# Routed expert layer: the first 128 picks of each expert in a tile of fixed weight address, overflow tiles through buffers that GpSimd fills

## What is computed

```python
def _moe(x2d, Wg, Wu, Wd, cw):
    g = jnp.einsum('th,ehi->eti', x2d, Wg)
    u = jnp.einsum('th,ehi->eti', x2d, Wu)
    a = jax.nn.silu(g) * u * cw.T[:, :, None]
    return jnp.einsum('eti,eih->th', a, Wd)
```

## Time and profile before

| | |
|---|---|
| median of 3 runs | 1508.38 us (1502.71 to 1508.43) |
| the profiled execution | 1497.24 us, its span 1495.4 us |
| PE busy over the span | 1141.3 us (76%) |
| DVE busy | 1062.4 us (71%) |
| ACT busy | 761.0 us (51%) |
| POOL busy | 647.7 us (43%) |
| mean granted clock of PE | 0.776 of full speed |

### The profile page before, as it was taken

One profiled execution on the slowest core, in us unless ns is written; L12 is line 12 of the kernel. 1 busy time (PEld: TensorE's weight loads), 2 busy tenths in 40 slices (PEclk: granted clock), 3 DMA queues, 4 the chain that ended last, 5 costly groups with the idle time before them and its releaser, 6 DMA issues.

```text
span 1495.4 us, 31927 instructions
## 1 busy us (share of the span) xinstructions
PE 1141.3 (76%) x11430; PEld 730.5 (49%) x11430; DVE 1062.4 (71%) x2436; ACT 761.0 (51%) x1506; POOL 647.7 (43%) x707
## 2 busy tenths in 40 slices
PE   5820677777763899996599982888888989996998
PEld 3510455555542322324478761555555665653565
DVE  7886122222257999996788859888888857658785
ACT  4446111111131889884245433989899943334432
POOL 5877000000053110400233335889988856774262
PEclk9955999999996555556699995555555579998999
DMA  9922222222231689894287723898998921111010
GB/s 360 410 122 96 70 65 64 62 65 64 57 124 43 127 176 183 171 182 108 64 211 198 200 54 80 129 149 151 153 152 152 143 61 59 53 44 43 11 33 29
DMA packets 401927, 176.41 MB, mean 118 GB/s; under 512 B 364912, under 2 KB 383600, under 8 KB 399344
## 3 DMA queue, kind: packets, MB, share of 16 engines
q1 hardware_dynamic: 395680, 158.79, 46.4%
q0 software_dynamic: 4800, 13.11, 2.9%
q10 hardware_dynamic: 1296, 2.48, 0.5%
HBM read 63.03 MB, written 22.81 MB: 57 GB/s over the span
## 4 chain that ended last, share of the span: by engine, by line
PE 35%; DVE 29%; POOL 13%; issue 11%; ACT 7%; DMA 5%; SPq 1%; ACTq 0%; POOLq 0%; DVEq 0%
PE s_all L1052 14%; DVE small L2524 8%; PE s_all L1183 5%; PE bank L1052 3%; PE s_all L1185 3%; POOL c_hi L958 3%; POOL slots L817 2%; POOL ffbuf L826 2%; PE s_all L1184 2%; DVE ffbuf L2322 2%; POOL c_lo L958 2%; PE s_all L1458 2%; POOL c_hi L956 2%; ACT ffbuf L1715 2%; DVE small L2527 1%
## 5 line engine op out<-in xcount | busy, mean ns | idle before, releaser
L1855 ACT ACTIVATE arena<-s_all,small 128x1024 int16<-128x1024 f32 x128 | 154.2, 1205 | 18.5 <-DVE small L2527 9.0
L2524 DVE TENSOR_REDUCE small<-s_all 128x1 f32<-128x1024 f32 x128 | 155.5, 1215 | 7.3 <-PE s_all L1458 7.2
L826 POOL DMA_INDIRECT ffbuf<-outs,small x32 | 31.9, 997 | 278.9 <-DMA outs<-xn 269.5
L1052 PE MATMUL s_all<-xt_hi,arena 128*128 128x512 f16 x512 | 142.9, 379 | 9.6 <-DVE xt_lo L2036 5.2
L2322 DVE SCALAR_TENSOR_TENSOR ffbuf<-s_all,ffbuf 128x256 f32<-128x256 f32 x63 | 26.7, 424 | 173.7 <-ACT ffbuf L1715 173.7
L1183 PE MATMUL s_all<-xt_hi,arena 128*128 128x128 f16 (+1 forms) x408 | 96.5, 239 | 56.6 <-issue 54.4
L1458 PE MATMUL s_all<-arena 32*128 32x512 f16 x256 | 130.1, 610 | 8.4 <-ACT arena L1855 3.4
L1715 ACT ACTIVATE ffbuf<-s_all 128x256 f32<-128x256 f32 x63 | 24.2, 384 | 195.3 <-PE s_all L1185 195.3
L1059 PE MATMUL s_all<-zeros 128*128 128x512 f16 x124 | 37.5, 463 | 110.9 <-DVE moments L2021 55.6
L1052 PE MATMUL bank<-arena 128*128 128x9 f16 (+1 forms) x2088 | 114.4, 191 | 8.0 <-DMA arena<-c_lo 4.4
L1052 PEld LDWEIGHTS bank<-arena 128*128 128x128 f16 x2088 | 100.4, 106 | 39.1 <-issue 12.7
(11 more groups left out here) (407 smaller groups left out, 3196.1 us busy)
## 6 DMA issues: line engine op xcount, KB each, us to landing
arena<-in_w_pairs SPq DMA_DIRECT2D x16, 1024.0 KB, 10.1
arena<-in_w_experts SPq DMA_DIRECT2D x48, 320.0 KB, 4.0
arena<-in_w_blocks SPq DMA_DIRECT2D x36, 384.0 KB, 3.1
slots<-zeros SPq DMA_DIRECT2D x1, 8064.0 KB, 31.5
outs<-xn SPq DMA_DIRECT2D x63, 128.0 KB, 1.7
arena<-in_w_attn SPq DMA_DIRECT2D x4, 512.0 KB, 10.3
arena<-arena SPq DMA_TRANSPOSE x122, 2.8
x<-in_x_in SPq DMA_DIRECT2D x2, 512.0 KB, 4.5
```

What stands on the lines that cost most here:

```text
L1052: m = nc.tensor.matmul(outp, lhs, rhs, start=(first and n == 0), stop=(last and n == len(steps) - 1), skip_group_check=True)
L1855: nc.scalar.activation(p2[n % P2_BUFS], s2[n % S2_BUFS], ACT.Exp, bias=small[:, 1, s * L2_UNITS + v:s * L2_UNITS + v + 1], scale=scale_g[s ...
L2524: nc.vector.tensor_reduce(small[:, 0, c:c + 1], s2[(g * L2_UNITS + v) % S2_BUFS], AX.X, ALU.max).then_inc(G[2, "chain"], 1)
```

## The change

The first 128 picks of expert e go to tile e (32 tiles, e = 0 to 31), picks past 128 to overflow tiles 32 to 62 (`OVER1` = 31). `ORDER1` sets the order in which the loop takes them: 0, 1, 32, 2, 33, 3, 34, ..., 31, 62; `PLACE1` is its inverse. Tile e reads its weights from a fixed place. For an overflow tile POOL reads the two addresses, and copies the expert's 2816 fp16 columns into one of two fixed buffers (`over1`): first those for gate and up (2 x 384 and 2 x 512 columns), then those for down (twice 2 x 256), each pair with an increment of `e1_copy` on which PE waits. PE has no `value_load` and no computed address in the loop any more; `mm3` orders the products otherwise (high by high for both halves, then high by low, then low by high). PE no longer waits for all of `we_lo` ahead of the loop, but pair by pair. DVE computes the slots with four more instructions on 128x256 values and one small copy. The number of tiles, their work on PE, ACT and DVE, and the DMAs stay as they are.

```diff
-TILES1 = T * TOP1 // P + E1 - 1
+OVER1 = T * TOP1 // P - 1
+TILES1 = E1 + OVER1
+ORDER1 = [0] + [tile for k in range(OVER1) for tile in (k + 1, E1 + k)]
+PLACE1 = {tile: n for n, tile in enumerate(ORDER1)}
...
+        over1 = [arena16[:, PAIRS1 * 2 * PW:PAIRS1 * 2 * PW + 2 * (LW + SW)],
+                 ffbuf[:, 6 * D:6 * D + LW + SW].bitcast(F16)]
...
@@ GpSimd, experts1, behind the scatter
+                pool.wait_ge(ex_rows, PUT1)
+                pool.wait_ge(we_lo, UNITS1)
+                pool.wait_ge(e1_route, 5)
+                for m in range(OVER1):
+                    large = pool.value_load(table[0:1, 0, m:m + 1], min_val=0, max_val=(PAIRS1 - 1) * 2 * PW + 2 * LW)
+                    small_ = pool.value_load(table[0:1, 1, m:m + 1], min_val=0, max_val=(PAIRS1 - 1) * 2 * PW + 4 * LW)
+                    parts = []
+                    for base, o, width in ((large, 0, LW), (small_, 2 * LW, SW)):
+                        parts.append((over1[m % 2][:, o:o + 2 * width].rearrange("p (a n) -> p a n", a=2),
+                                      arena16[:, bass.ds(base, 2 * width)].rearrange("p (a n) -> p a n", a=2)))
+                    if m > 1:
+                        pool.wait_ge(ex_u, PLACE1[E1 + m - 2] + 1)
+                    for dst, src in parts:
+                        k = nc.gpsimd.tensor_copy(dst[:, :, 0:dst.shape[2] - D], src[:, :, 0:dst.shape[2] - D])
+                    k.then_inc(e1_copy, 1)
+                    if m > 1:
+                        pool.wait_ge(ex_y, PLACE1[E1 + m - 2] + 1)
+                    for dst, src in parts:
+                        k = nc.gpsimd.tensor_copy(dst[:, :, dst.shape[2] - D:], src[:, :, dst.shape[2] - D:])
+                    k.then_inc(e1_copy, 1)
...
@@ TensorE, experts1
-                pe.wait_ge(e1_route, 5)
                 pe.wait_ge(we_first, 12 * SPLIT1_POOL)
-                pe.wait_ge(we_lo, UNITS1)
                 pe.wait_ge(ex_rows, PUT1)
                 fill(10)
...
+                def weights_of(n):
+                    tile = ORDER1[n]
+                    if tile >= E1:
+                        w = over1[(tile - E1) % 2]
+                        return w[:, 0:2 * LW], w[:, 2 * LW:2 * (LW + SW)]
+                    o = tile // 2 * 2 * PW
+                    return (arena16[:, o + tile % 2 * 2 * LW:o + (tile % 2 + 1) * 2 * LW],
+                            arena16[:, o + 4 * LW:o + 2 * PW])
 
                 def gate_up(n):
-                    large = pe.value_load(table[0:1, 0, n:n + 1], min_val=0, max_val=(PAIRS1 - 1) * 2 * PW + 2 * LW)
-                    small_ = pe.value_load(table[0:1, 1, n:n + 1], min_val=0, max_val=(PAIRS1 - 1) * 2 * PW + 4 * LW)
-                    offs[n] = (large, small_)
+                    tile = ORDER1[n]
+                    if tile >= E1:
+                        pe.wait_ge(e1_copy, 2 * (tile - E1) + 1)
+                    elif tile // 2 >= SPLIT1_POOL and tile % 2 == 0:
+                        pe.wait_ge(we_lo, 3 * (tile // 2 - SPLIT1_POOL + 1))
                     pe.wait_ge(land5[n % XT1_BUFS], 16 * (n // XT1_BUFS + 1))
...
                 def down(n):
+                    if tile >= E1:
+                        pe.wait_ge(e1_copy, 2 * (tile - E1) + 2)
                     pe.wait_ge(ex_hl, n + 1)
...
@@ VectorE, experts1
+                link(nc.vector.tensor_copy(shift1[:, :], bank[7][:, P:P + E1]))
+                link(nc.vector.scalar_tensor_tensor(out=slot1, in0=cum, scalar=float(P), op0=ALU.is_ge, op1=ALU.mult,
+                                                    in1=shift1[:, :].unsqueeze(1).broadcast_to([P, NT, E1])))
+                link(nc.vector.scalar_tensor_tensor(out=slot1, in0=cum, scalar=1.0, in1=slot1, op0=ALU.add, op1=ALU.add))
+                link(nc.vector.tensor_tensor(slot1, slot1, tri[:, 2 * P:2 * P + E1].unsqueeze(1).broadcast_to([P, NT, E1]),
+                                             ALU.add))
+                link(nc.vector.tensor_tensor(key1, slot1, pick1, ALU.mult))
```

More of the change, by code:

```diff
@@ L53 @@
 Y1_BUFS = 4
-C1_BEFORE, C1_INCL, C1_STEP, C1_IOTA = 0, E1, 2 * E1, 2 * E1 + 2
-C1_COLS = C1_IOTA + 2 * E1
+C1_BEFORE, C1_UPTO, C1_SHIFT, C1_TILE, C1_STEP = [n * E1 for n in range(5)]
+C1_COLS = C1_STEP + 2
 EXPERTS = {0: [2] * 4, 5: [8] * 2, 7: [1] * 8 + [4]}
@@ L527, in build @@
         e1_add = sem("e1_add")
+        e1_copy = sem("e1_copy")
         G = {}
```

82 lines of the change are left out of this document (39 added, 43 removed).

## The result

The kernel after takes **1375.63 us** (median of 4 runs, 1374.14 to 1377.89) against 1505.7 of the kernel before, measured beside it: a ratio of 0.914 (95% interval 0.911 to 0.917), 130 us less. The forecast was made to a kernel before of 1508.4 us; beside the kernel after it took 2.7 less.

What follows compares the result with a forecast made beforehand. PE was taken to bound the loop at about 2.28 us a tile: 261 us before, less 144 after, less 1 in front, gives 116 us gain, from 1508.4 to 1392 us; range 1376 to 1437.

Steps and rivals of the forecast that it cites:

- The start of the loop as the key: First gate matmuls after the fills: 55 ns each without register instructions between them, and tile 0's loads cost nothing there.
- the rival of 1437 us: PE's matmuls not paced at 55 ns but at 85: 3.0 us a tile, loop 189 us, gain 71; chance 5%.
- the two breaks: PE's pauses per tile: 0.13 us between gate and down matmuls, 0.13 to 0.2 at the tile's start.
- The low end of the range: Breaks of 0.05 us on PE, 2.1 us a tile, loop 132 us, 1380, less 4 us for scatter: 1376.
- it costs where the engine's queue is empty: PE's register loads: not tied to an idle engine; the gap ahead of a tile was 1.26 us.
- POOL's loads at the lower end: POOL's register loads hidden behind its copies, costing nothing in a round of 3.08 us; upper end 4.8 us.
- The 0.86 for sharing: POOL's copies may lose 2 x 0.43 us a round to DVE's `hidden_low` over SBUF: 3.94 us, under 4.56.
- 0.25 us more for `hidden_low`: DVE's low part waits on average about half a POOL copy; DVE's round becomes 1.95 us a tile, under 2.28.
- The rival in which DVE bounds: Each `hidden_low` behind a whole gate copy: 2.4 to 2.7 us a tile, gain 96, 1412 us; chance 9%.
- 0.5 to 1 us of loss: Ahead of the loop: two added DVE instructions with two SBUF inputs run beside `pairs1`, the start of POOL's chain.
- 1.5 us a tile fits into 2.28: SP's queue in the loop: its 1.5 us a tile fits PE's new tile; DMA share rises from 0.25 to 0.46.
- The slower rival: POOL's round makes the kernel slower from 8.4 us on; at 9 us the loop takes 280, time 1528; chance 4%.

Runs made afterwards that it cites:

- `no_copies`: The kernel after without POOL's loads and copies, overflow tile m using the fixed weights of expert m: 1375.02 us, ratio 0.913.

## Why the prediction was right, and where it fell short

- **The start of the loop as the key**: right. 55 ns a matmul held for 63 tiles, 24 x 0.056 at a granted clock of 1.00. The rule of the Trainium skill ("TensorE: Matmul & The Clock Gate", section "Back-to-back issue gap"), some 81 ns a matmul at 128 columns with weight loads, which was the rival of 1437 us, is refuted here: each of these matmuls has its own weight load.
- **The term that was mis-sized: the two breaks.** The prediction kept "the break of 0.13", "which is a semaphore wait and stays", and one of "0.13 to 0.2" at the tile's start: 2.28 us a tile. Both are 0. The tile is 2.00, and that is 63 x 0.28 = 17.6 us, less 1.6 of gaps that SP's queue leaves and 1.8 at the gather: 14.2, near the 14 by which the sum was short. They had been the sequencer at work: between gate_up and down it has a wait instruction of 51 ns and a register instruction of 46. Once the sequencer is ahead, the array doesn't see them, and the semaphore is met before the array gets there. The low end of the range allowed them 0.05 and so missed by 0.4 us; 0.4 us is less than the scatter of the runs, and of the 16.4 us between forecast and time 2.7 are that the kernel before ran faster beside the kernel after.
- **Why the sum came out near all the same:** it took 2.0 us of gate matmuls, 0.7 of down and 1.26 of gap as three stretches of one engine. In truth it was one stretch of the sequencer of 4.1 us, beside 2.0 of array. The reading "it costs where the engine's queue is empty" was right, but the queue was empty through the whole tile, and the register instructions are 54 to 57 of the 130 us: taking out the loads alone gives 73, and taking out the register instructions alone leaves the loads nearly free (8 us).
- **POOL's loads at the lower end:** right. The sequencer was a whole round ahead; put in the open they cost 1.31 us a round and 12 us in all. The copies were to take 3.08 us and take 2.87 undisturbed, some 3.3 beside DVE. The price of a column had been taken in part from a cast out of fp32; it held all the same, 829 ns for 768 columns and 1042 for 1024. The 0.86 for sharing was an upper bound; up to 0.4 was measured.
- **DVE:** 0.25 us more for `hidden_low` were expected, 0.33 measured (750 against 425 ns). All 49 longer low parts end 0.27 to 0.28 us behind a copy's end. This bears out the rule of the Trainium skill ("SBUF — State Buffer", section "Who interferes with whom") that such an instruction and a GpSimd instruction that reads SBUF exclude each other. The rival in which DVE bounds did not come about: `no_copies` takes the same time with the low parts at 425 ns.
- **Front and end:** 0.5 to 1 us of loss was foreseen in front and 1.6 gained in the traces; as the first gate matmul scatters by 3 to 4 us from trace to trace, neither is shown. (DVE has four instructions more in all, three on 128x256 values and the small copy; the fourth such replaces one that was there.) The end was taken as unchanged and lost 1.8 in these two traces, by later landings.
- **SP:** "1.5 us a tile fits into 2.28" became 1.86 for most tiles and 2.06 in the mean, against 2.00. It does not quite fit, and costs PE 1.6 us of idle time in this trace. The DMA share in the loop is 0.56, where 0.46 was expected.
- **A slip of the sum:** a tile of 2.1 to 2.35 us gives 1380 to 1396 by the prediction's own terms, not 1382 to 1400. Nothing hangs on it.
- **The slower rival** named POOL's round as the mechanism and 8.4 us a round as the point. In the kernel's own order it was 2.9 to 3.3. In another order a ring through both engines made it 7.2 us a single tile, and the kernel slower than before; the prediction had priced only POOL's own work, not how its two waits lie in PE's order.

## What to carry to other kernels

PE was two machines in these runs, a sequencer and an array, and the slower one set the pace; before pricing a gap, add up what the sequencer has to do per tile, register instructions for computed addresses included: a PE that gets its matmuls 85 instead of 55 ns apart shows as busy, and only the spacing of the starts, or the share of the weight loads, tells. When the bound moves, add up every queue anew against the new tile, with its long cases: here SP's was the next. Work that another engine is to prepare costs nothing while its round fits between two uses and its waits form no ring with the consumer's order: check what stands behind each wait on both engines. An experiment meant to remove one thing must be read in the order of its instructions first, since the builder may remove another with it.

## What the runs showed of the hardware

- A register load on PE takes the sequencer 295 to 315 ns and 150 more for its register instruction, on POOL 285 to 293 and 152; a pair, with its checks, 1.3 to 1.35 us. Where the array had work queued, all but 0.13 to 0.18 us of a pair was hidden.
- A computed operand address costs some 0.11 us of PE's sequencer per matmul that needs a new one, though its own row says 46 ns; 30 matmuls with fixed addresses, with their weight loads, cost it 0.82 us.
- A DVE instruction with two SBUF inputs and a POOL copy within SBUF did not run at once: 49 of 63 such DVE instructions ended 0.27 to 0.28 us behind a copy's end, at up to 1168 instead of 425 ns.
- SP's issue of the same store took 0.57 us where stores and transposes stood back to back, 0.32 where the queue had pauses, and 0.33 on ACT's queue. Its issue of a transposing load took 1.2 us, but 1.3 to 2.6 in 15 of 63 cases.
- PE's granted clock was 0.70 where it idled 3.4 us in every tile of 7.2, and 1.00 where it idled 0.9 in every 3.1.
